# SP fetches its own rows 32 at a time, right after loading their numbers

## What is computed

```python
x = x + ((1 + eps) * h + segment_sum(h[src] * edge_weight[:, None], dst))          # L0
x = x + L1(h)     # three GRU steps; each: m = h @ conv[i]; agg = segment_sum(w_e * m[src], dst); h = gru(agg, h)
x = x + relu(zeros.at[dst].add(alpha[rel] * (h @ W_rel[rel])[src]) .at[dst].add((h @ update)[dst]))   # L2
x = x + (h + mean over edges of h[dst], summed by src) @ W.T + b                     # L3
```

## Time and profile before

| what | us |
|---|---|
| median of three runs | 6547.37 |
| lowest and highest | 6542.28, 6547.39 |
| the profiled execution | 6555.57 |
| its span | 6553.8 |
| POOL busy | 4766.0 (73%) |
| DVE busy | 3827.2 (58%) |
| PE busy (matmul) | 3315.8 (51%) |

### The profile page before, as it was taken

How to read it: one execution, slowest core, us unless ns; L and a number is a source line. 1 busy time by engine, 2 the same in 40 slices (tenths; PEclk the granted TensorE clock), 3 DMA queues, 4 the chain that set the end, 5 groups by cost and what they waited for, 6 DMA issues and landing times.

```text
span 6553.8 us, 107755 instructions
## 1 busy us (share of the span) xinstructions
PE 3315.8 (51%) x13560; PEld 2693.6 (41%) x13560; DVE 3827.2 (58%) x13371; ACT 858.8 (13%) x2167; POOL 4766.0 (73%) x5006
## 2 busy tenths in 40 slices
PE   3444445444447555555755554696444444444444
PEld 3333334333334444444444543343333333333333
DVE  6767666666666656656666664454454444444445
ACT  1000001000002111111211110143333333000000
POOL 6777776777774677777677777675777776777775
PEclk9555556555557666666876665696555555555556
DMA  5434442333332222222122222154222222222222
GB/s 140 111 107 110 110 110 74 74 75 75 75 75 53 53 54 54 54 54 53 46 54 53 53 54 54 48 212 140 54 53 54 53 54 55 54 54 54 54 54 59
DMA packets 276003, 471.96 MB, mean 72 GB/s; under 512 B 99701, under 2 KB 181882, under 8 KB 269035
## 3 DMA queue, kind: packets, MB, share of 16 engines
q0 software_dynamic: 156176, 306.05, 19.1%
q1 hardware_dynamic: 84091, 85.05, 3.8%
q10 hardware_dynamic: 35040, 73.87, 3.6%
HBM read 389.33 MB, written 77.27 MB: 71 GB/s over the span
## 4 chain that ended last, share of the span: by engine, by line
POOL 41%; issue 20%; DMA 13%; SPq 12%; PE 11%; DVE 3%; ACT 1%; DVEq 0%; POOLq 0%; ACTq 0%
POOL G L665 40%; DMA G<-h_rows,ix_src 11%; PE ps L769 10%; SPq L540 9%; SPq L532 3%; DMA G<-h_rows 1%; PE ps L826 1%; DMA t_rows<-G 0%; DVEq L1223 0%; DMA G<-t_rows,pos 0%; DVE HNA L1234 0%; SPq L551 0%; DVE bst L1151 0%; DVE M L1214 0%; ACT HG L1703 0%
## 5 line engine op out<-in xcount | busy, mean ns | idle before, releaser
L665 POOL DMA_INDIRECT G<-h_rows,ix_src x3860 | 3703.3, 959 | 1296.5 <-issue 1051.2
L769 PE MATMUL ps<-G,M 128*128 x10000 | 2554.6, 421 | 3081.0 <-SPq L551 2182.9
L769 PEld LDWEIGHTS ps<-G,M 128*128 128x128 f32 x10000 | 2168.9, 310 | 3431.6 <-issue 3425.9
L1234 DVE TENSOR_TENSOR HNA<-HNA,ps 128x128 f32 (+1 forms) x3328 | 957.8, 288 | 1359.8 <-PE ps L769 1338.8
L1214 DVE TENSOR_SCALAR M<-irow,rel,w_l 128x128 f32<-128x128 f32 x3328 | 1207.1, 365 | 180.7 <-issue 174.2
L665 POOL DMA_INDIRECT G<-t_rows,pos x770 | 740.9, 962 | 260.0 <-issue 228.8
L1234 DVE TENSOR_TENSOR HTA<-HTA,ps 128x129 f32 x840 | 243.3, 290 | 518.1 <-PE ps L769 509.7
L1803 ACT ACTIVATE sorting<-sorting,pk 128x128 f32<-128x128 f32 x784 | 250.6, 390 | 1446.9 <-DVE sorting L1409 1444.2
L769 PE MATMUL ps<-sorting 128*128 128x128 f32 x1568 | 435.1, 374 | 0.5 <-ACT sorting L1803 0.3
L1881 ACT ACTIVATE G<-G,pk 128x128 f32<-128x128 f32 x782 | 311.7, 402 | 679.1 <-DMA G<-t_rows,pos 678.7
L1234 DVE TENSOR_TENSOR X<-X,ps 128x128 f32 x832 | 239.1, 287 | 230.0 <-PE ps L769 223.6
(11 more groups left out here) (270 smaller groups left out, 2150.7 us busy)
## 6 DMA issues: line engine op xcount, KB each, us to landing
G<-h_rows SPq DMA_DIRECT2D x7680, 0.5 KB
G<-h_rows,ix_src POOLq DMA_INDIRECT x3860, 2.6
t_rows<-G SPq DMA_DIRECT2D x49, 1024.0 KB, 4.0
HTA<-in_edge_attr_n ACTq DMA_DIRECT2D x50, 500.0 KB
HTA<-in_edge_attr ACTq DMA_DIRECT2D x50, 500.0 KB
G<-t_rows SPq DMA_DIRECT2D x1536, 0.5 KB
sorting<-q_flat ACTq DMA_DIRECT2D x98, 196.0 KB
G<-t_rows,pos POOLq DMA_INDIRECT x770, 2.5
```

What stands on the lines that cost most here:

```text
L665: return nc.gpsimd.indirect_dma_start(to, None, table, bass.IndirectOffsetOnAxis(ap=ix, axis=0))
L769: return nc.tensor.matmul(dst, lhsT, rhs, start=start, stop=stop, skip_group_check=True)
L1234: V.tensor_tensor(to, to, ps[:, u % SLOTS, 0:n], ALU.add).then_inc(s_add, 1)
```

## The change

In `arrivals` the call of `fetch` moves under the condition that a new load of numbers has been made, and there it runs over four values of `q` in one go. The rows are the same 128, in the same order and from the same registers; they are issued in four groups of 32, each right behind its load, and no longer in sixteen groups of eight. Between the loads SP now has arrivals alone. The L2 loop is as before.

```diff
                             if q * ROWS_A_QUAD % RD == 0:
                                 row = row_numbers(listed, c, j, q, table.shape[0])
-                            fetch(k, j, q, table, row)
+                                for ahead in range(q, q + RD // ROWS_A_QUAD):
+                                    fetch(k, j, ahead, table, row)
                         one(c, j * RING + BY_ROW)
```

## The result

| what | before | after |
|---|---|---|
| median, us (nine runs of each on one chip) | 6544.52 | 6562.82 |
| lowest to highest | 6536.45 to 6547.39 | 6558.12 to 6568.56 |
| the profiled execution | 6555.57 | 6562.82 |
| its span | 6553.8 | 6561.0 |

The changed kernel is slower by a factor of 1.0029, with an interval from 1.0019 to 1.0039, or 18.3 us between the medians. The two profiled executions lie only 7.2 us apart. The one of before is 11 us above its median of 6544.52: its stage between pass 3 and the L2 pass lasts 300.8 us and its L2 pass 991, where the profile after has 296.6 and 987.1, and the change touches neither.

What follows compares the result with a forecast made beforehand. POOL bounds the kernel, one gather every 1.25 us and hardly ever waiting for data. Terms 9.7 + 1.5 + 1.5 + 0 + 1 = 13.7 us on a median of 6547.37 give 6561.1 us; range 6547 to 6577.

Steps and rivals of the forecast that it cites:

- The sign and the cause: Whole kernel slower by 13.7 us, because SP reports nothing for 15.2 us from each load instead of 5.3.
- the three places that it named: POOL's gate at tile 64 of pass 0, its gate at tile 68 of later passes, and the pass ends.
- the threshold where SP becomes the bound: Rival, 9%: long bursts slow SP's issues; from 0.52 us a row SP costs more than POOL; +260 us at 0.55.
- The size: Whole kernel: 13.7 us added, bounds 9 to 20 us.
- The price of the parts: SP: 225 ns an issue, 0.41 us a row, load 2.05 us, so 15.2 us silent from a load.
- Tile 64 of pass 0: Round 0 ends 6.0 us later, PE resumes near 126; less 1.1 us cover, POOL stalls 4.9 us (2 to 7).
- The ends of the passes: After tile 755: pass 0 ends 9.7 us later, 4.9 of them stall; passes 1 and 2 1.5 each; pass 3, L3 0.
- Rival 1: Pass tails are covered because the stage behind waits for something else; about +6 us, 6553; 13%.
- The gates at tile 68: Passes 1, 2, 3 and L3: POOL waits for 56 steps, 0.3 us in pass 1; 1 us for all four (0 to 3).
- The row waits: SP's 88.5 us in 60 waits for its own rows, tile 63, go away; counted as no gain.
- PE was given nothing back: Pass 0 stall: from step 32 on DVE is the limit in both kernels, so PE recovers none of the delay.

Runs made afterwards that it cites:

- two half-changed kernels: Against the kernel before, rows go out 32 at a time in pass 0 alone: 6554.49 us; in the three L1 passes and L3 alone: 6548.21 us.
- 12, 12, 8 cut: Against the kernel before, groups of 12, 12, 8 and 0 rows follow each load, the last row issued three arrivals earlier: 6545.35 us, 1.0007.

## Why the prediction was right, step by step

**The sign and the cause: right.** Sparing the three places that it named gives back all of the loss, and the threshold where SP becomes the bound was crossed by an experiment at the price that it gives. A cost of 13.7 us was forecast, 18.3 measured.

**The size: in part luck.** 18.3 us is a net figure. In the profile after, the places that the sum names cost 25.4 us: 6.8 at tile 64, 8.0 at tiles 68 and 69 of the later passes, and 10.6 in the five tails. The forecast had 13.7 for these, 20 at the most. What brings the result back are two gains that the sum counted at nothing: the gathers of pass 1 take 3.2 to 4.6 us less apart from the stall in them (973.3 against 976.5 to 977.9), and the stage behind pass 1 takes 2.2 to 3.0 us less. Both are treated below.

**The price of the parts: right.** An issue takes 225 ns, and the burst in pass 1 12.92 us, as forecast. Three quarters of the bursts (177 of 240) take some 13.25 us. In those behind tile 51 of the four other passes one issue comes 0.3 us late. The silence from report to report is so 15.3 us behind tile 51 of pass 1 and 15.7 in the others, where 15.2 was forecast; 0.16 of the difference lies between the report and the load.

**Tile 64 of pass 0: right in its mechanism, 1.9 us short.** The forecast was a restart at about 126 and a stall of 4.9 us; PE resumes at 126.39, and the stall is 6.8 us. The shift of PE's last matmul of round 0 is as forecast (6.0; 105.64 against 99.75 is 5.9). Three small things were left out of the sum:
- What PE resumes behind is the last addition, and it moves by 6.6 us: DVE ends 1.4 us behind PE after twelve steps in a row, and 0.7 before.
- POOL comes to tile 64 0.9 us sooner in the profile after (tile 62 starts at 133.59, before at 134.50), so the shift that it sees is 7.5 us.
- The cover was 0.7 us and not 1.1. The gather starts 0.77 us behind the end of the step that its gate waits for (step 51 ends at 140.85, tile 64 starts at 141.62; the same 0.77 with groups of 16 and with the bursts in pass 0 alone), where the sum had 0.3. Before, step 51 ended at 134.25, so the gate would have let the gather start at 135.03, and it started at 135.74.

7.5 less 0.7 is the stall of 6.8 us.

**The ends of the passes: right in place, small in size.** The tail of pass 0 grew by 6.1 us (forecast 4.8), those of passes 1 and 2 by 2.0 and 2.2 (1.5 each), that of pass 3 not at all (0), that of L3 by 0.4 (0). Pass 0 ended at 1044.47, forecast near 1042. Rival 1, that these tails are covered by the stage behind, falls with the kernel that spares the last bursts: its time follows them.

**The gates at tile 68: the term that was mis-sized.** The forecast was 1 us for four passes, 3 at the most. The profile has 0.5, 2.7, 1.2 and 3.6 us in passes 1, 2, 3 and L3, 8 in all, and sparing them gave some 9 us back. I had worked out a stall of 0.3 us in pass 1 and written that the other passes have the same geometry. Pass 1 was the one to be right, and by luck too: the 0.77 us below were not in its sum, and the arrival of tile 51 came 0.65 us sooner behind the first gather than before. Where a cover is nearly zero, everything small counts in full:
- in all four passes the gather of tile 68 starts 0.77 us behind the end of the 56th step, where the sum had 0.3;
- the silence is 0.1 us longer in pass 1 and 0.5 in the others, and it starts when the arrival of tile 51 happens to be reported, 66.3, 67.1, 67.6 and 67.6 us behind the first gather in passes 1, 2, 3 and L3;
- in passes 2 and 3 the four steps take 2.5 us and not 2.1, since PE has matmuls of its side work between them;
- behind the gate wait POOL can lose more than the wait. In pass 2 and L3 the next gather started after 1.44 us of idle time and not 0.30, another 1.1 us each that no row of before showed. L3's is the row at 5626.39 above, and this is tiles 68 and 69 of pass 2 (the 56th step ends at 2236.55):

```profile
2237.32 0.94 POOL L666 DMA_INDIRECT G<-h_rows,ix_src  x1 [1.89 <-SPq L551]
2239.70 0.94 POOL L666 DMA_INDIRECT G<-h_rows,ix_src  x1 [1.44 <-issue]
```

A cover that is worked out in one pass as -0.3 us should have been worked out in all four, with a spread of a microsecond, since a negative one costs and a positive one pays nothing back.

**The row waits: half right.** I wrote that the 88.5 us of SP's waiting for its own rows would go without a gain. No gain came, but 47.6 us of them stayed, in 51 places. Behind the last burst SP reports a backlog of eleven tiles within a microsecond or so, and is then at tile 63 soon after its last row has been sent. What I had overlooked is that SP comes late to the arrivals in front of tile 63 as well, and so to tile 63 sooner behind its rows.

**The profiles side by side.** Pass by pass, the two half-changed kernels serve as the kernel before, each in the passes where it has groups of eight. From the first gather to the last addition, pass 0 takes 976.6 us with groups of eight and 989.8 after, passes 1 to 3 and L3 982.7, 984.5, 979.8 and 981.2 against 981.9, 986.8, 984.9 and 985.0. That is +13.2, -0.8, +2.3, +5.1 and +3.8. The stage behind pass 1 took 3.0 us less (81.6 against 84.6). The sum is 20.6, beside 18.3 to 19.5 by the medians. With the profile before itself (976.3, 984.1, 983.0, 982.4 and 982.9, and 83.8 for the stage) it is 17.5. Single passes differ by up to 3 us between two profiles with the same groups, so only the sums are worth comparing.

**A gain that was not forecast.** This last term goes with TensorE's clock. The windows of the stage behind pass 1, before and after (the granted clock is the third last column):

```profile
2060.00:2143.80 83.80, 77.12 (x254) 40.00 (x254) 53.91 (x86) 38.53 (x66) 0.00 (x0) 0.95 0.13 39
```

```profile
2069.60:2151.20 81.60, 74.94 (x254) 38.96 (x254) 53.89 (x85) 38.50 (x66) 0.03 (x1) 0.98 0.13 40
```

The stage is 2.2 us shorter in this pair, and so is PE's busy time in it (77.12 to 74.94), at a clock of 0.98 in place of 0.95. It goes with the burst behind tile 755 of pass 1, the last one, and not with those before it. With this burst the stage takes 81.6 us in four kernels, 83.3 in the one that spares round 0 and 82.9 with loads of four numbers. The seven kernels without it take 83.6 to 84.6, also the two that keep 45 and 42 of the 48 long bursts of pass 1. (Loads of two numbers, where SP sets the pace, have 91.9 and are left out here.) This is the one that spares only the last bursts:

```profile
2065.32:2149.82 84.50, 77.67 (x254) 40.20 (x254) 53.91 (x85) 38.53 (x66) 0.04 (x1) 0.94 0.12 39
```

These are single profiles of each kernel. In the prediction PE was given nothing back; this is the one place found where a shorter busy time of PE shortened the kernel.

## What to carry to other kernels

A queue that both moves data and reports arrivals has a longest silence, and that, beside its total work, is what a reordering changes: list who waits behind it and with how much cover (a gate, the start of a chain, the end of a phase), and keep long bursts away from these few places alone; in the steady state their net cost was not measurable here until the queue's total passed that of the engine that sets the pace. Compare the sum of the single places with the net result as well: here 25 us of losses and 7 of gains that nobody had counted made up 18. Where a cover comes out near zero, work it out for every occurrence and count a spread of a microsecond against it. A wait that is long in the profile of a queue is a gain only if an engine that sets the end stands behind it: sending its DMA earlier bought nothing here, and spreading two rows behind every arrival bought 0.1%.

## What the runs showed of the hardware

- **With the bursts TensorE's granted clock is higher.** Over the same 930 us of L3, before, after, and with bursts in pass 0 alone (columns as in the earlier trace rows):

```profile
5560.00:6490.00 930.00, 402.70 (x1600) 350.52 (x1600) 397.00 (x1600) 0.00 (x0) 703.43 (x744) 0.52 0.21 54
```

```profile
5560.00:6490.00 930.00, 367.03 (x1596) 318.87 (x1597) 393.74 (x1592) 0.00 (x0) 700.14 (x743) 0.63 0.21 54
```

```profile
5560.00:6490.00 930.00, 405.65 (x1602) 351.99 (x1603) 398.30 (x1604) 0.00 (x0) 703.10 (x744) 0.52 0.20 54
```

The same number of matmuls in the same time, but in clumps behind each silence: the mean granted clock goes from 0.52, almost always the 1.2 GHz level, to 0.63, and PE's busy time falls by 9% (402.70 to 367.03). Groups of 16 give 0.60, the 12, 12, 8 cut 0.55, two rows at a time 0.52. It is worth nothing inside these passes, where POOL sets the pace.
- **A load of numbers into SP's registers is no fixed cost.** 32 numbers take 2.03 us, four 0.299, two 0.472 each time, so two cost more than four in one instruction. Why is open.
- **Behind a gate wait POOL sometimes loses an extra 1.1 us** (1.44 us of idle time in place of 0.30). In the changed kernel, its half in the later passes, those that spare round 0 or the last bursts, and the ones with loads of four and of two numbers, it came at tile 69 of pass 2 and of L3, each time, and never in passes 0, 1 and 3, though the waits there reached 7.09 us in the changed kernel. So the length of the wait doesn't decide it; what does is open.
- **A gather starts 0.77 us behind the end of the step that its gate waits for**, wherever POOL stood at the gate on steps in the changed kernel: tile 64 of pass 0 and tile 68 of passes 1, 2, 3 and L3. Where it doesn't stand there, 0.30 us lie between two gathers.
- **Pass 1's gathers** took, from the first to the last, 971.5 to 974.9 us with groups of 2, 16 or 32 rows (976.1 with loads of four numbers, 2.2 us of them its stall at tile 68), and 976.5 to 977.9 with groups of 8 or 12. The time between the gathers is the same to within 1 us (234.5 us before and with two rows, 235.0 after); more of them take longer than 0.94 us themselves. Over 1.05 us take 62 before, 58 and 54 in the two others with groups of 8 or 12, 41 in the changed kernel, 35 with groups of 16 and 34 with two rows. In this pass DVE sorts beside the gathers, and the two may get in each other's way differently; no run separates that, and it stays open.
